# Block quantisation of a state-space and FP4 layer: the rounding constant formed on ScalarE instead of VectorE

## The reference

```
u  = silu(conv3(x));  B, C = split(u @ W_bc + b_bc)          # 16 states each
dt = softplus((u @ W_dt + b_dt) @ W_dtp + b_dtp)
h_t = exp(A*dt) * h_(t-1) + B*u*dt;   y = sum over the states of C * h
x1 = layernorm(x + y + x*Dcoeff)
q(v): per block of 16: scale = max|v|/6, v/scale to the nearest of 0, .5, 1, 1.5, 2, 3, 4, 6, times scale
h  = silu(q(x1) @ q(w_gate)) * (q(x1) @ q(w_up))             # 352 wide
out = layernorm(x1 + q(h) @ q(w_down))
```

## Time and profile before

| | |
|---|---|
| median of 3 runs | 389.12 us |
| the 3 runs | 383.5, 389.15, 389.12 us |
| profiled execution: its own time | 383.09 us |
| profiled execution: its span | 381.3 us |
| busy in the span: PE, DVE, ACT, POOL | 70%, 84%, 60%, 76% |
| instructions: PE, DVE, ACT, POOL | 1130, 364, 505, 171 |
| mean granted TensorE clock | 0.898 of full speed |
| chain that ended last: PE, ACT, DVE, POOL | 31%, 19%, 17%, 13% of the span |

### The profile page before, as it was taken

How to read it: one execution, slowest core, us unless ns; L and a number is a source line. 1 busy time by engine, 2 the same in 40 slices (tenths; PEclk the granted TensorE clock), 3 DMA queues, 4 the chain that set the end, 5 groups by cost and what they waited for, 6 DMA issues and landing times.

```text
span 381.3 us, 3999 instructions
## 1 busy us (share of the span) xinstructions
PE 266.0 (70%) x1130; PEld 122.8 (32%) x1130; DVE 319.7 (84%) x364; ACT 228.2 (60%) x505; POOL 289.7 (76%) x171
## 2 busy tenths in 40 slices
PE   2457659678856879688868786878687664772683
PEld 1123122223311335233613261336222432261372
DVE  4875979999999998989899998899889997356670
ACT  3453755955596459755995488657964664053234
POOL 0092655687588999899889998998899899955542
PEclk9859898799989999799999998899969895897798
DMA  3740460190028002720192009200730001000001
GB/s 63 159 117 1 92 157 2 31 203 14 2 58 192 1 0 59 163 55 2 22 200 55 2 0 202 74 2 2 172 75 2 0 0 28 0 3 0 28 2 55
DMA packets 19246, 21.86 MB, mean 57 GB/s; under 512 B 6096, under 2 KB 15128, under 8 KB 19224
## 3 DMA queue, kind: packets, MB, share of 16 engines
q1 hardware_dynamic: 18504, 21.05, 24.4%
q10 hardware_dynamic: 720, 0.56, 0.8%
HBM read 2.72 MB, written 2.10 MB: 13 GB/s over the span
## 4 chain that ended last, share of the span: by engine, by line
PE 31%; ACT 19%; DVE 17%; POOL 13%; issue 12%; SPq 3%; DMA 2%; ACTq 1%; POOLq 0%; DVEq 0%
PE ps_prep L1216 7%; DVE states L957 7%; PE ps_b L1223 5%; DVE db L941 4%; POOL product L700 3%; ACT c_rep L541 3%; SPq L422 3%; ACT ps_decay L465 3%; PE ps_y L1182 3%; PE ps_prep L1203 3%; POOL qh_norm L721 2%; POOL qh_norm L716 2%; PE ps_f L1248 2%; POOL hq L759 2%; DMA dt_rep<-dtx 2%
## 5 line engine op out<-in xcount | busy, mean ns | idle before, releaser
L700 POOL TENSOR_TENSOR product<-states,c_rep 128x1024 f32<-128x1024 f32 x64 | 151.0, 2364 | 30.6 <-DVE states L957 28.8
L465 ACT ACTIVATE ps_decay<-dt_rep,aneg 128x512 f32<-128x512 f32 x128 | 87.4, 692 | 39.6 <-DVE states L957 36.5
L941 DVE SCALAR_TENSOR_TENSOR db<-ps_b,bbc_rep,dt_rep 128x2048 f32<-128x2048 f32 x31 | 72.5, 2338 | 10.7 <-PE ps_b L1223 8.3
L957 DVE TENSOR_TENSOR_SCAN states<-ps_decay,states,db 128x512 f32<-128x512 f32 x64 | 78.9, 1259 | 2.4 <-POOL product L700 2.4
L957 DVE TENSOR_TENSOR_SCAN states<-ps_decay,db 128x512 f32<-128x512 f32 x64 | 75.4, 1203 | 0.4 <-ACT ps_decay L465 0.2
L1216 PE MATMUL ps_prep<-u_feat,wbc_rep 128*128 128x512 f32 x56 | 37.1, 749 | 21.0 <-ACT c_rep L541 20.8
L1223 PE MATMUL ps_b<-u_feat,wbc_rep 128*128 128x512 f32 x64 | 40.5, 719 | 15.5 <-DVE db L941 15.4
L1248 PE MATMUL ps_f<-gate_t,xq_t 128*128 128x352 f32 x64 | 30.1, 554 | 13.7 <-DVE hidden L1012 8.1
L1182 PE MATMUL ps_y<-product,gather 128*32 128x512 f32 x256 | 37.1, 654 | 2.9 <-POOL product L700 2.9
L579 ACT ACTIVATE gate_tanh<-ps_f 128x352 f32<-128x352 f32 x32 | 14.8, 464 | 37.6 <-PE ps_f L1248 37.6
L541 ACT ACTIVATE c_rep<-ps_prep,bbc_rep 128x512 f32<-128x512 f32 x28 | 19.4, 693 | 16.6 <-PE ps_prep L1216 16.0
(11 more groups left out here) (172 smaller groups left out, 502.9 us busy)
## 6 DMA issues: line engine op xcount, KB each, us to landing
dt_rep<-dtx SPq DMA_DIRECT2D x124, 128.0 KB, 2.4
x_tok<-in_L_attn_x SPq DMA_DIRECT2D x8, 256.0 KB, 3.1
out<-y_out SPq DMA_DIRECT2D x8, 256.0 KB, 2.4
dt_rep<-dtx ACTq DMA_DIRECT2D x4, 128.0 KB, 3.7
hidden<-in_L_ffn_w_down SPq DMA_DIRECT2D x1, 176.0 KB, 3.4
x_feat<-in_L_attn_x SPq DMA_DIRECT2D x8, 0.5 KB, 2.7
hidden<-in_L_ffn_w_gate SPq DMA_DIRECT2D x1, 128.0 KB, 2.7
hidden<-in_L_ffn_w_up SPq DMA_DIRECT2D x1, 128.0 KB, 2.6
```

The source lines that it names most:

```text
L465: nc.scalar.activation(ps_decay[BANK_OF[k]][:], dt_rep[p][:, c, 0, :], ACT.Exp, scale=aneg[:, c, m:m + 1]).then_inc(decay_done, 1)
L700: nc.gpsimd.tensor_tensor(product[:, j % PRODUCTS], states[p][:, first:first + 2, :], over(c_rep[p][:, j // SET_PAIRS, :], 2), ALU.mult).t ...
L941: nc.vector.scalar_tensor_tensor(out=db[m % DB][:], in0=over(ps_b[:], QUADS), scalar=bbc_rep[:, 0, m:m + 1], in1=dt_rep[p][:, :, 1, :], op ...
L957: nc.vector.tensor_tensor_scan(out=states[p][:, k % ring, :], data0=ps_decay[BANK_OF[k]][:], data1=db[k // QUADS % DB][:, k % QUADS, :], i ...
```

## The change

The square stays where it is. Behind it ACT now waits for its own result and adds the offset with a second instruction, an `Identity` with the bias `magic_low` (a new 128x1 tile that POOL fills at the start). DVE's add-and-minimum falls away for x and h, in the steps and in the tail; the upper limit `MAGIC_HIGH` is gone, and the two constants are chosen anew. The square of x goes straight into `qx_magic`, so `x_square` is not needed. POOL waits for the same semaphores `x_magic_done` and `h_magic_done`, which ACT now raises. In the tail DVE's two rounding operations (L903, L905 before) become `code_x` and `code_h`, both still on DVE.

```diff
-SQUARE_SCALE = 2.0 ** 11 / 2.14
-MAGIC_LOW, MAGIC_HIGH = 1.03125 * 2.0 ** 22, 7.0 * 2.0 ** 22
+SQUARE_SCALE = 2.0 ** 11 * 0.184 ** 0.5
+MAGIC_LOW = 1.1015625 * 2.0 ** 22
...
-    "dve x quant": {0: (7, False), 1: (7, False), 2: (8, True), 5: (10, False)},
-    "dve h quant": {0: (3, False), 1: (3, False), 2: (4, False), 5: (9, False)},
+    "dve x quant": {0: (7, False), 1: (7, False), 2: (8, True)},
+    "dve h quant": {0: (3, False), 1: (3, False), 2: (4, False)},
...
             def square_x(f):
                 act.wait_ge(x_norm_done, f.at(1, 1))
                 if f.beyond(1):
-                    act.wait_ge(x_magic_done, f.at(1))
-                nc.scalar.activation(x_square[:, 0:TILES * D // BLOCK, 0:BLOCK], blocked(qx.norm[:]), ACT.Square,
-                                     scale=SQUARE_SCALE).then_inc(x_square_done, 1)
+                    act.wait_ge(xq_done, f.at(1))
+                nc.scalar.activation(qx.magic[:], qx.norm[:], ACT.Square, scale=SQUARE_SCALE).then_inc(x_square_done, 1)
+                act.wait_ge(x_square_done, f.at(1, 1))
+                nc.scalar.activation(qx.magic[:], qx.magic[:], ACT.Identity, bias=magic_low[:]).then_inc(x_magic_done, 1)
...
             def square_h(g):
 
                 act.wait_ge(h_norm_done, g.at(1, 1))
                 nc.scalar.activation(qh.magic[:], qh.norm[:], ACT.Square, scale=SQUARE_SCALE).then_inc(h_square_done, 1)
+                act.wait_ge(h_square_done, g.at(1, 1))
+                nc.scalar.activation(qh.magic[:], qh.magic[:], ACT.Identity, bias=magic_low[:]).then_inc(h_magic_done, 1)
...
-                if n == 9:
-                    square, to = (x_square[:, :, 0:BLOCK], blocked(b.magic[:, 0:width + BLOCK])) if b is qx \
-                        else (b.magic[:], b.magic[:])
-                    return nc.vector.tensor_scalar(to, square, MAGIC_LOW, MAGIC_HIGH, ALU.add, ALU.min)
```

More of the change, by code:

```diff
@@ L203, in build @@
         eps = sb("eps", [128, TILES])
+        magic_low = sb("magic_low", [128, 1])
         center = sb("center", [128, 128])
@@ L256, in quant_buffers @@
                          [sb(f"{name}_{what}", [128, lines * ROW]) for what in ("scale", "inv")],
-                         [sb(f"{name}_norm", [128, width]), sb(f"{name}_magic", [128, lines * ROW * BLOCK], bf16)])
+                         [sb(f"{name}_norm", [128, width]), sb(f"{name}_magic", [128, width], bf16)])
         qx = quant_buffers("qx", TILES * D)
         qh = quant_buffers("qh", TILES * INNER)
-        x_square = sb("x_square", [128, TILES * D // BLOCK + 1, BLOCK + 2], bf16)
         def flat(t):
@@ L685, in _ @@
             nc.gpsimd.memset(eps[:], EPS).then_inc(masks, 1)
-            pool.wait_ge(masks, 4)
+            nc.gpsimd.memset(magic_low[:], MAGIC_LOW).then_inc(masks, 1)
+            pool.wait_ge(masks, 5)
             orders = [Order(pool, norm_order[n], POOL_NORM) for n in range(2)]
@@ L977, in u_of, with code_x, code_h, gate @@
                     op0=ALU.add, op1=ALU.mult).then_inc(u_done, 1)
-            def gate(f, slot, early, coded=False):
+            def code_x(f):
+                dve.wait_ge(x_magic_done, f.at(1, 1))
+                order_g.mark(quant_op(6, None, None, qx, TILES * D))
+                order_g.need()
+                quant_op(7, None, None, qx, TILES * D).then_inc(x_code_done, 1)
+            def code_h(g):
+                dve.wait_ge(h_magic_done, g.at(1, 1))
+                order_q.mark(quant_op(6, None, None, qh, TILES * INNER))
+                order_q.need()
+                quant_op(7, None, None, qh, TILES * INNER).then_inc(h_code_done, 1)
+            def gate(f, slot, early):
                 src = flat(x1[f.first % X1][:])
@@ L1018, in gate, with quant @@
                                             ALU.mult).then_inc(hidden_done, 1)
-            def quant(g, slot, early, coded=False):
+            def quant(g, slot, early):
                 for n in [n for n, place in AT["dve h quant"].items() if place == (slot, early)]:
@@ L1026, in quant @@
                             dve.wait_ge(hq_done, g.at(1))
-                    elif n == 5:
-                        dve.wait_ge(h_square_done, g.at(1, 1))
                     else:
                         order_q.need()
-                    last = quant_op(9 if n == 5 else n, flat(hidden[:]), None, qh, TILES * INNER, HIDDEN_SCALE)
+                    last = quant_op(n, flat(hidden[:]), None, qh, TILES * INNER, HIDDEN_SCALE)
                     if n == 2:
                         last.then_inc(h_inv_done, 1)
-                    elif n == 5:
-                        last.then_inc(h_magic_done, 1)
                         assert order_q.n == DVE_QUANT, order_q.n
-                        if coded:
-                            dve.wait_ge(h_magic_done, g.at(1, 1))
-                            order_q.mark(quant_op(6, None, None, qh, TILES * INNER))
-                            order_q.need()
-                            quant_op(7, None, None, qh, TILES * INNER).then_inc(h_code_done, 1)
                     else:
@@ L1079, in tail @@
                 for place in sorted(set(AT["dve x quant"].values()), key=in_step):
-                    gate(f, *place, True)
-                for place in sorted({h_places[n] for n in (5,)}, key=in_step):
-                    quant(g, *place, True)
+                    gate(f, *place)
+                code_x(f)
+                code_h(g)
                 def op(n, i, needed):
```

14 lines of the change are left out of this document (1 added, 13 removed).

## The result

The changed kernel takes 398.35 us in the median of 6 runs (396.45 to 400.5). The kernel before, measured beside it, takes 387.16 us in the median of 6 (383.5 to 389.15). The ratio is 1.036, with a 95% interval of 1.031 to 1.040. It leaves out executions in a slower state, which the kernel before enters now and then, and so is larger than the ratio of the two medians (1.029). The profiled execution takes 397.39 us (span 395.6) against 383.09 us before, so 14.3 us are to be found in the two traces.

The account below looks back on a forecast made before the run. ACT, late ahead of the C copies in slots 8 to 13, was taken as the bound, with DVE having time over. Terms of 11.7 us on 383.1 gave 394.8, plus 3.0 for run spread: about 398 us, range 389 to 405.

Parts of the forecast that it names:

- The price of the additions: New ACT instructions behind the squares: 1.48 us for h, 0.72 for x; 2.28 us of ACT's list with waits.
- Steps 3 and 5: Later C copies on ACT delay PE's spread of B and DVE's wide product by 2.1 to 2.4; 2.3 us each.
- Step 4: PE expected to lose its 2.4 GHz clock: 42.0 us against 39.2, so 2.8 us, at least 1.2.
- the first rival: PE's low clock lasts through spread of B and state sum: some 1.5 us more in four steps; chance 0.19.
- Step 2: No variance here; POOL's 1.56 us wait for DVE's x constant shrinks, so -0.3 us, bounds 0 and -1.6.
- The tail: After the last step, both additions delay DVE's rounding of x from 346.12 to 347.98: 1.9 us later.
- The sum: Whole kernel: terms total 11.7 us, giving 394.8 on the profiled execution; 3.0 added for slower runs, about 398.
- The check on DVE's wait: DVE's idle time before the wide product of slot 14 grows from about 1.2 to over 4 us, steps 3 to 6.
- The other signs: Whole kernel: ACT's busy time grows some 16 us, DVE's falls some 6; POOL's x sum comes about 1.2 later.
- Hidden additions: ACT's 11.7 idle us a step absorb the new work, leaving 383.1 us (386 with half the run spread); chance 0.06.
- DVE as the bound: DVE's list of slots 8 to 15 decides each step, so 4.8 us go: 378.3 us; chance 0.04.
- POOL as the one that ends the step: POOL's order, delayed by the variance, costs 1.2 us in each of steps 3 to 6; 389.9 us, chance 0.20.

Follow-up runs that it names:

- no_add: Changed kernel without the two additions on ACT, so the offset is left out of the computation; 382.88 us, ratio 0.996.
- h_after_var: Changed kernel with the h addition moved one place in ACT's list, behind the variance but still ahead of the first C copy; 397.44 us, ratio 1.030.
- after_warm: Changed kernel with PE computing the first C piece of steps 3 to 6 three times more to fill its gap; 390.46 us, ratio 1.015.
- x_dve: Changed kernel with the x addition back on DVE in slot 10, the h addition still on ACT; 395.85 us, ratio 1.031.
- h_dve: Changed kernel with the h addition back on DVE in slot 9, the x addition still on ACT; 389.21 us, ratio 1.013.
- before_warm: Kernel before, with PE computing the first C piece of steps 3 to 6 twice more to fill its gap; 385.28 us, ratio 1.001.
- late_h: Changed kernel with the h addition moved on ACT from slot 8 to slot 11, behind the fourth C copy; 392.59 us, ratio 1.022.
- late_all: Changed kernel with h square and h addition behind ACT's fourth C copy, x addition behind the second; 386.31 us, ratio 1.005.
- before_late2: Repeat run of the kernel before with ACT's h square behind the third C copy and DVE's add-and-minimum in slot 12; 381.63 us, ratio 0.988.

## Why the prediction was right

The forecast was 398 us and slower; 398.35 us was measured. Point by point:

- **The bound.** That ACT is the late engine from slot 8 to 11 and DVE has time over held. no_add shows the worth of DVE's relief at 0.4%, and h_after_var takes the variance out as the way of the loss while the clock is low, so that the C copies and what stands behind them are left. What the prediction didn't split is lateness and clock: at full clock DVE and POOL take up most of the C copies' delay, and 0.8 to 0.9 us of the step is left (step 3 of after_warm); the rest comes with the low clock.
- **The price of the additions.** The forecast had 1.48 and 0.72 us, from the square and from the price of a bias tile in the rows. Measured are 1.47 (all seven) and 0.72 (all eight), starting 0.02 to 0.04 us behind the square's end. Against DVE's 0.50 us for the addition and the minimum of h that is a factor of 2.9; the 2.8 of the prediction came from the square, which reads float32. PE's second C piece moved by 1.51 us within step 5 (from 16.38 to 17.89 us behind the step's start), where 1.52 was forecast.
- **Steps 3 and 5.** Forecast 2.3 each, measured 2.0 and 2.4. All of PE's second to fourth pieces were at the low level there, the case with PE last, for which 2.4 was worked out. The second C copy, the spread and the wide product of step 5 all moved by 2.45 us or 2.46.
- **Step 4.** The low clock came as forecast, in place of 1.00. The term was mis-sized: 3.9 us, not 2.8. The low level lasted through the spread of B and the sum of the states behind it. In step 5 the sum of the states (L1173) took 1.00 us on the chain. PE's timeline of step 4:

```profile
207.08 1.92 PE L1214 MATMUL ps_b<-u_feat,wbc_rep 128*128 128x512 f32 x2
...
208.93 1.94 PE L1173 MATMUL ps_y<-product,gather 128*32 128x512 f32 x8
```

  This is what the first rival said (the low clock lasts longer). It came true in part: in step 4 and, with the same 1.87 us on the chain, in step 6 (2.9 us in place of 2.3), but not in 3 and 5. The size of this term also rests on a chance: step 4 was the one step of the kernel before that kept its clock in the profiled execution, and in no_add, whose lists on ACT and PE are the same, step 4 lost it.
- **Step 2.** This term failed: forecast -0.3, measured 1.7. I reasoned on POOL's wait for DVE's x constant, which did shrink (from 1.56 to 0.28 us), and took the low clock to be a matter of steps 3 to 6. But the gaps ahead of the second and third C piece grew from 0.78 to 1.44 and 1.33 us there too, the clock fell in the third piece (1.53 us, then 2.08, above), and DVE waited 1.98 us for the spread of B before its wide product. In the kernel x_dve, without the x addition, the four pieces of step 2 took 1.12 or 1.13 us and the step 38.9 us; in h_dve, without the h addition, the clock fell in the fourth piece and the step took 39.7. It took both additions to make the 1.7.
- **The tail.** Forecast 1.9, measured 1.3. DVE's and POOL's timelines:

```profile
360.88 0.69 DVE L902 TENSOR_TENSOR qx_norm<-qx_norm,qx_magic 128x512 f32<-128x512 f32 x1 [5.72 <-ACT qx_magic L588]
...
362.38 2.37 POOL L744 TENSOR_TENSOR xq<-qx_norm,qx_scale 128x512 f32<-128x512 f32 x1 [6.08 <-DVE qx_norm L904]
```

  DVE now waits 5.72 us for ACT's constant, in place of 3.47. POOL's `xq` took 2.37 us beside DVE's float32 operations, where it took 1.27 before. What won back part of it is POOL's root of the variance (L714, L710 before): it took 1.01 us in place of 2.38, now that DVE's rounding of h, beside which it ran before, had ended, and so released the copy `y_out` only 1.5 us later than before.
- **The sum.** 11.7 us forecast, 14.3 us found in the profiled execution. The 3.0 us that I put on top, for executions at other clocks, made up for it: the right total owes something to two errors of opposite sign. The changed kernel's median is only 1.0 us above its profiled execution, since its clock falls in nearly every step and there is little left to vary.
- **The check on DVE's wait.** "From about 1.2 to over 4 us before the wide product" held in sum (4.15 us) and not in place: it is spread over three waits, since the decays of slots 12 and 13 stand behind C copies in ACT's list and POOL's product frees the ring.
- **The other signs.** ACT's busy time grew by 15.3 us, about the 16 forecast. DVE's fell by 4.8, as in the prediction's sum and not by the "some 6" of its signs. POOL's sum for x came 0.8 us later within step 5 (20.9 us behind its start, 20.1 before), not 1.2, since its own wait of 0.39 us was gone.
- **The rivals.** Hidden additions and DVE as the bound are refuted by x_dve and no_add. POOL as the one that ends the step was wrong for the changed kernel as it ran (h_after_var) and right where the clock was kept: in the kernel before (before_warm) and in step 3 of after_warm, where 0.8 to 0.9 us was left of the 1.2 that the rival gave it.

## What to carry to other kernels

Work given to an engine with idle time can cost as much as its own duration if it lands ahead of something that others wait for (15 us for 16 us of work here); ask not only how full the engine is but what stands behind the new instruction in its list. The cheapest test of that is to move the instruction: h_after_var and late_h separate cause from cause without any change of the work. When several things move at once, as in late_all, compare with a kernel that shares all moves but one. And look whether what was there already stands in the wrong place: here the square itself, moved behind the third C copy, gave 1.2 to 1.3%, where the change lost 3.6%.

## What the runs showed of the hardware that was not expected

- The low clock cost about 2% of the changed kernel (1.036 against 1.015 with PE's gaps filled), and 1.9 us in a single step (42.02 against 40.11 us in step 3). In the kernel before, filling the gap kept 2.4 GHz throughout steps 3 to 5 and shortened steps 3 to 6 by 2.1 us in the profile, but gained nothing that could be measured in the whole (1.001).
- Whether the clock falls is not settled by one gap, but it goes with the gaps. Taking steps 3 to 6 of all fourteen profiled executions by the longest gap that PE had ahead of its second to fourth C piece, and counting a step when one of these pieces took longer than 1.13 us:

| longest gap, us | steps | clock fell in |
|---|---|---|
| 0.8 | 20 | 2 |
| 1.3 | 8 | 6 |
| 2.1 | 16 | 13 |
| 3.5 or 3.6 | 12 | 12 |

- The same gaps gave both outcomes: 2.10 us in steps 3, 5 and 6 of the kernel before with a fall and in step 4 without, and after_warm, with the 3.6 us gap filled to 1.0, fell in three steps of four, later in the chain. What decides it in one execution stays open here.
- Short gaps can be enough: in step 2 of the changed kernel the clock fell in the third piece behind gaps of 1.44 and 1.33 us, and in step 3 of before_late2 in the third piece behind gaps of 0.83 and 0.78 us.
